# A hand-ordered setup of a fused attention and expert kernel: its steps and first loads in another order

## The reference

```python
mod = (silu(c) @ wmod).reshape(8, 6, 1, 256)       # six vectors a batch
sa, ca, ga, sb, cb, gb = (mod[:, i] for i in range(6))
ga = (2 * (ga >= 0) - 1) * maximum(abs(ga), 0.25)  # the gates, gb alike
h = layernorm(x) * (1 + ca) + sa
x = x + ga * attention(h, ...)   # q = (h w_dq^T) w_uq^T and a rotated part through w_qr,
                                 # k, v = (h w_dkv^T) through w_uk, w_uv, rotated k = h w_kr^T;
                                 # causal softmax over 512 keys, then w_out
h = layernorm(x) * (1 + cb) + sb
x = x + gb * ffn(h, ...)         # top 8 of 32 experts merged into 8 groups of width 96
```

## Time and profile before

| | us |
|---|---|
| median of 3 runs (lowest, highest) | 1097.45 (1093.78, 1107.73) |
| the profiled execution's own time | 1096.97 |
| its span in the trace | 1095.0 |
| PE busy | 1026.2 (94%) |
| DVE busy | 771.5 (70%) |
| ACT busy | 401.1 (37%) |
| POOL busy | 412.7 (38%) |

### The profile page before, as it was taken

One profiled execution on the slowest core, in us unless ns is written; L12 is line 12 of the kernel. 1 busy time (PEld: TensorE's weight loads), 2 busy tenths in 40 slices (PEclk: granted clock), 3 DMA queues, 4 the chain that ended last, 5 costly groups with the idle time before them and its releaser, 6 DMA issues.

```text
span 1095.0 us, 24777 instructions
## 1 busy us (share of the span) xinstructions
PE 1026.2 (94%) x9744; PEld 730.9 (67%) x9744; DVE 771.5 (70%) x1516; ACT 401.1 (37%) x723; POOL 412.7 (38%) x349
## 2 busy tenths in 40 slices
PE   6979989999999989999899999999999998999778
PEld 4646667766677667766677666776677666776456
DVE  5767687585957868677885859678686777857344
ACT  3334533254314443145332543144431453314310
POOL 1526442264505353154422644054441544226100
PEclk9989999999999999999999999999999999999979
DMA  6220000200002000200002000020002000010000
GB/s 191 58 88 2 2 1 1 68 2 2 1 4 67 2 1 1 69 2 2 1 1 69 2 2 1 2 69 2 1 1 69 2 2 1 1 49 2 1 1 20
DMA packets 22232, 23.59 MB, mean 22 GB/s; under 512 B 6314, under 2 KB 20138, under 8 KB 22130
## 3 DMA queue, kind: packets, MB, share of 16 engines
q1 hardware_dynamic: 22130, 22.02, 6.6%
HBM read 17.80 MB, written 4.21 MB: 20 GB/s over the span
## 4 chain that ended last, share of the span: by engine, by line
PE 82%; DVE 11%; issue 4%; ACT 2%; POOL 1%; DMA 1%; POOLq 0%; DVEq 0%; SPq 0%; ACTq 0%
PE ring L1131 17%; PE ring L981 12%; PE ring L982 10%; PE ring L983 10%; PE ring L1203 8%; PE av L1147 7%; PE ring L1107 6%; PE ring L1098 3%; DVE mcol L863 2%; DVE xr L902 1%; PE ring L1115 1%; PE ring L1192 1%; DVE prod L839 1%; PE av L1160 1%; PE ring L1042 1%
## 5 line engine op out<-in xcount | busy, mean ns | idle before, releaser
L672 ACT ACTIVATE pt<-ring 128x384 f32<-128x384 f32 (+1 forms) x384 | 170.9, 532 | 326.2 <-PE ring L1131 289.7
L562 POOL TENSOR_SCALAR_AFFINE_SELECT pt<-pt 128x512 f32<-128x512 f32 x128 | 79.4, 635 | 409.6 <-ACT pt L672 409.6
L863 DVE TENSOR_REDUCE mcol<-ring 128x1 f32<-128x128 f32 (+3 forms) x512 | 212.3, 483 | 19.3 <-PE ring L1107 18.1
L839 DVE TENSOR_TENSOR prod<-ring,table 128x1024 f32<-128x1024 f32 x128 | 155.4, 1219 | 93.1 <-PE ring L983 92.5
L1131 PE MATMUL ring<-rows 32*128 32x512 f32 (+3 forms) x3072 | 175.9, 330 | 9.4 <-ACT pt L672 4.9
L1131 PEld LDWEIGHTS ring<-rows 32*128 32x128 f32 x3072 | 130.4, 184 | 60.6 <-issue 35.0
L553 POOL TENSOR_TENSOR rows<-prod,rows 128x1024 fp32r<-128x1024 f32 x64 | 152.5, 2393 | 36.3 <-ACT rows L652 36.3
L546 POOL TENSOR_TENSOR prod<-prod 128x512 f32<-128x512 f32 x64 | 82.5, 1290 | 134.3 <-DVE prod L839 133.7
L652 ACT ACTIVATE rows<-prod 128x1024 fp32r<-128x1024 f32 x64 | 67.0, 1060 | 60.2 <-PE ring L1131 39.3
L1147 PE MATMUL av<-pt,vals 128*17 128x512 f32 (+3 forms) x1024 | 85.3, 439 | 3.2 <-POOL pt L562 3.2
L1131 PE MATMUL ring<-cont 32*128 32x512 f32 (+3 forms) x1024 | 85.6, 319 | 0.0
(11 more groups left out here) (162 smaller groups left out, 1624.4 us busy)
## 6 DMA issues: line engine op xcount, KB each, us to landing
xn<-x_dram SPq DMA_DIRECT2D x8, 512.0 KB, 4.1
...
dn<-wu_t_dram SPq DMA_DIRECT2D x1, 640.0 KB, 10.1
...
```

The source lines that it names most:

```text
L672: sc.activation(pt[:, PT_AT[n] + h * w:PT_AT[n] + (h + 1) * w], ps[:, 0:w], ACT.Exp, scale=SCALE).then_inc(exp_ready.sem, 1)
L839: ve.tensor_tensor(prod[:, s % PROD, :, :], ps[:, :].unsqueeze(1).broadcast_to([P, 2, S]), table[:, :, :], ALU.mult).then_inc(rotated.sem, 1)
L863: last = ve.reduce_max(mcol[:, q, h * HR + HD:h * HR + HD + 1], ps[:, at:at + (q + 1) * P], AX_X)
```

## The change

The setup list becomes one table, and three things move. `spread` goes to the front; the sixteen steps and the rest are in a new order, with `fuse.0` behind the first two `rope` steps, both `values` last, and `fuse.4`, `fuse.5` among the `maxima`. The gates' five DVE instructions become two steps, `gates_out` (the two that read PSUM) and `gates_end` (the other three), far apart. The loads of the query weights are divided in columns 0 to 511 and the rest, the rest behind the small loads with a semaphore of its own. The two tiny `groups` loads go to places two and three of SP's queue, ahead of `c_t` and `wmod`. SP waits for the PE part of `gates` where it waited for DVE's read of it. No arithmetic changes.

```diff
@@ the list (a line or two of it; the moves stand below) @@
-latent.0 latent_hi.0 latent_lo.0 fuse.1 rope.0000 rotate.0000 rope.0001 rotate.0001 combine.000 kcon.00 kcon_hi.00
...
+modulate1.01 low1.01 latent.0 latent_hi.0 latent_lo.0 rope.0000 rope.0001 rotate.0000 rotate.0001 combine.000
+gates_out. fuse.0 hi.000 fuse.1 rope.0010 rotate.0010 lo.000 rope.0011 rotate.0011 split_uv. combine.001 kcon.00
...
-def setup_steps():
-    out = [("silu",), ("stats1", 0), ("pow1", 0), ("norm1", 0), ("mod",), ("split_d",), ("split_k",), ("turn1", 0, 0), ("turn1", 0, 1),
-           ("gates",), ("modulate1", 0, 0), ("low1", 0, 0), ("modulate1", 0, 1), ("low1", 0, 1), ("fuse", 0), ("split_uv",)]
-    return out + steps_of(SETUP_ORDER)
...
             sp.dma_start(idx_sb[:, :], chosen).then_inc(ld_idx, 16)
+            for copy in range(2):
+                sp.dma_start(grp_i[copy * NX:(copy + 1) * NX, :], groups).then_inc(ld_idx, 16)
             sp.dma_start(ct[:, :, :], c_t.rearrange("(c p) b -> p c b", p=P)).then_inc(ld_mod, 16)
...
-            sp.dma_start(wu_main, wu_t[0:P, :]).then_inc(ld_q, 16)
-            sp.dma_start(wu_rest, wu_t[P:CQ, 0:NG * NROPE]).then_inc(ld_q, 16)
-            sp.dma_start(wu_rest_con, wu_t[P:CQ, NG * NROPE:NQ]).then_inc(ld_q, 16)
+            sp.dma_start(wu_main[:, 0:512], wu_t[0:P, 0:512]).then_inc(ld_q, 16)
+            sp.dma_start(wu_rest[:, 0:512], wu_t[P:CQ, 0:512]).then_inc(ld_q, 16)
...
-                sp.dma_start(grp_i[copy * NX:(copy + 1) * NX, :], groups).then_inc(ld_small, 16)
             sp.dma_start(gw_st, gw_t.rearrange("(c p) n -> p c n", p=P)).then_inc(ld_small, 16)
+            sp.dma_start(wu_main[:, 512:], wu_t[0:P, 512:NQ]).then_inc(ld_rest, 16)
+            sp.dma_start(wu_rest[:, 512:], wu_t[P:CQ, 512:NG * NROPE]).then_inc(ld_rest, 16)
+            sp.dma_start(wu_rest_con, wu_t[P:CQ, NG * NROPE:NQ]).then_inc(ld_rest, 16)
...
-            sp.wait_ge(gates_read, 1)
+            sp.wait_ge(full_sem, full_value(0, "setup", PLACES["setup"][0][("gates",)]))
...
-                    elif kind == "gates":
+                    elif kind == "gates_out":
...
                         ve.sem_inc(gates_read, 1)
+                    elif kind == "gates_end":
                         chain(ve.scalar_tensor_tensor(gates_abs, gates_abs, -1.0, gates_abs,
...
                         if step[1] == 0:
-                            pe.wait_ge(ld_q, 80)
+                            pe.wait_ge(ld_q, 64)
+                        if step[1] == EC:
+                            pe.wait_ge(ld_rest, 48)
...
+                        if isinstance(b, int) and b == 0 and g == 2 and t == 1:
+                            pe.wait_ge(fuse_read, len(FUSE))
...
                         if part == "setup":
-                            pe.wait_ge(fuse_read, len(FUSE) if g else 2 * EC)
+                            pe.wait_ge(fuse_read, 2 * EC)
```

More of the change, by code:

```diff
@@ L68, in steps_of @@
         kind, args = token.split(".")
-        out.append((kind, *map(int, args)))
+        out.append((kind, *(int(i) for i in args)))
     return out
 SETUP_ORDER = """
-latent.0 latent_hi.0 latent_lo.0 fuse.1 rope.0000 rotate.0000 rope.0001 rotate.0001 combine.000 kcon.00 kcon_hi.00
-kcon_lo.00 rope.0010 rotate.0010 rope.0011 rotate.0011 hi.000 lo.000 combine.001 fuse.2 fuse.3 hi.001 lo.001
-rope.0100 rotate.0100 qcon.00 qcon_hi.00 qcon_lo.00 rope.0101 rotate.0101 combine.010 values.00 values_out.00
-values.01 values_out.01 kcon.01 kcon_hi.01 kcon_lo.01 hi.010 maxima.000 reduce.000 lo.010 rope.0110 rotate.0110
-maxima.001 reduce.001 rope.0111 rotate.0111 combine.011 maxima.002 reduce.002 fuse.4 fuse.5 qcon.01 qcon_hi.01
-qcon_lo.01 shift.00 shifted.00 hi.011 lo.011 spread. split_ffn.0 split_ffn.1
+spread. silu. stats1.0 pow1.0 split_d. norm1.0 mod. split_k. turn1.00 turn1.01 gates. modulate1.00 low1.00
+modulate1.01 low1.01 latent.0 latent_hi.0 latent_lo.0 rope.0000 rope.0001 rotate.0000 rotate.0001 combine.000
+gates_out. fuse.0 hi.000 fuse.1 rope.0010 rotate.0010 lo.000 rope.0011 rotate.0011 split_uv. combine.001 kcon.00
+kcon_hi.00 kcon_lo.00 rope.0100 rope.0101 fuse.2 fuse.3 hi.001 lo.001 rotate.0100 rotate.0101 combine.010 qcon.00
+qcon_hi.00 qcon_lo.00 maxima.000 reduce.000 fuse.4 hi.010 rope.0110 rotate.0110 rope.0111 rotate.0111 combine.011
+lo.010 gates_end. maxima.001 reduce.001 fuse.5 split_ffn.0 kcon.01 kcon_hi.01 kcon_lo.01 qcon.01 qcon_hi.01
+qcon_lo.01 hi.011 lo.011 split_ffn.1 maxima.002 reduce.002 shift.00 shifted.00 values.00 values_out.00 values.01
+values_out.01
 """
@@ L144, in ring_places @@
     return place, n
-SETUP, FIRST, LAST = setup_steps(), steps_of(BODY_ORDER), steps_of(LAST_ORDER)
+SETUP, FIRST, LAST = steps_of(SETUP_ORDER), steps_of(BODY_ORDER), steps_of(LAST_ORDER)
 PLACES = {}
@@ L251, in block_program @@
         av = ctx.enter_context(nc.psum_tensor("av", [P, 512], F32))
-        ld_wo, ld_d, ld_mod, ld_q, ld_k, ld_tab, ld_small, ld_ffn, ld_down, ld_idx = (
-            sem(n) for n in ("ld_wo", "ld_d", "ld_mod", "ld_q", "ld_k", "ld_tab", "ld_small", "ld_ffn", "ld_down", "ld_idx"))
+        ld_wo, ld_d, ld_mod, ld_q, ld_rest, ld_k, ld_tab, ld_small, ld_ffn, ld_down, ld_idx = (
+            sem(n) for n in ("ld_wo", "ld_d", "ld_mod", "ld_q", "ld_rest", "ld_k", "ld_tab", "ld_small", "ld_ffn", "ld_down", "ld_idx"))
         x_loaded = Count(sem("x_loaded"), 1, 16)
@@ L325, in block_program @@
         cst_ready = sem("cst_ready")
-        N_SMALL = 7
+        N_SMALL = 5
         def full_value(b, part, place):
@@ L466, in _ @@
                       .then_inc(ld_tab, 16)
-            sp.wait_ge(ld_idx, 16)
+            sp.wait_ge(ld_idx, 48)
             sp.wait_ge(mod_read, 1)
-            sp.wait_ge(gates_read, 1)
+            sp.wait_ge(full_sem, full_value(0, "setup", PLACES["setup"][0][("gates",)]))
             chosen_at = [sp.value_load(idx_sb[0:1, g:g + 1], min_val=0, max_val=NX - 1) for g in range(G)]
@@ L757, in program @@
                         last.then_inc(mod_ready, 1)
-                    elif kind == "gates":
-                        ps = wait_full(ve, b, part, step)
+                    elif kind == "gates_out":
+                        ps = wait_full(ve, b, part, ("gates",))
                         ve.wait_ge(keys_split, 1 + EC)
@@ L770, in program @@
                     elif kind == "spread":
-                        ve.wait_ge(ld_small, 16 * N_SMALL)
+                        ve.wait_ge(ld_idx, 48)
                         ve.wait_ge(pool_setup, 4)
```

## The result

The change makes the kernel slower: **1112.08 us** median of 20 runs (1107.14 to 1113.85) against 1097.42 (1092.20 to 1107.92, 20 runs). The ratio is 1.0111, 95% interval 1.0086 to 1.0137: under 2%, but clear of no change. The profiled execution took 1113.46 us with a span of 1111.4, against 1096.97 and 1095.0: 16.4 us more of span.

What follows compares the result with a forecast made beforehand. PE was taken to bound the kernel, busy 1026 of 1095 us, so only setup waits and low clock could change. Setup balance +2.5 plus 0.5 for the clock, +3 us on 1096.97, gave 1100.0, range 1093 to 1106.

Steps and rivals of the forecast that it cites:

- DVE's queue: Setup, first maxima to shift: 17.1 us of DVE work plus 1.5 of waits ends at 68.1; PE stands still 7.5 us.
- the clock of the give-back: PE's lower clock behind the new pauses and at the front: 0.5 us taken for both, 0 to 2.6 kept.
- The loads: Kernel start: two `groups` issues ahead of `wmod` make PE begin at 10.1, +1.1 us.
- The front: Early setup: `latent` starts at 22.5, 2.8 us earlier, and `combine.000` at 28.0, 6.7 us earlier.
- The give-back: Setup up to `maxima.000`: PE pauses of 2.1, 2.9 and 1.6 us turn the 6.7 us lead into a 1.4 loss.
- takes some 1.6 (the pair shown 1.12 ...): `split_uv` on DVE ahead of `kcon.00`: pair 1.12 us plus two smaller operations estimated at 0.5, so PE waits 2.9.
- 67 to 70: Sign of a wrong forecast: DVE's last setup reduction, forecast to end at 68.1 us, ending outside this range.
- 2 us of waits: Sign of a wrong forecast: DVE's queue behind `maxima.000` having more waits than this; 1.5 us was forecast.
- The clock behind the shift: Behind PE's 7.5 us pause: a 1.2 GHz stretch as long as before's 6.8 us, losing 3.2, so no difference.
- If the body, not the setup, moved by more than 3 us: Sign of a wrong forecast: the unchanged work behind the setup was expected to keep its length.
- third rival: Loop: clock falls in all eight batches, not four, adding four 1.6 us stretches, +6.4; 1103 to 1108 us, chance 0.15.
- first two rivals: Clock does not fall or falls half as long, 1096 to 1098, chance 0.15; 6.7 us lead kept, 1085 to 1091, 0.1.

Runs made afterwards that it cites:

- o0: The changed code and loads with the setup list of the kernel before: 1099.52 us, ratio 1.0024 to the kernel before.
- a1: The changed kernel with only `split_uv` moved, to right behind `low1.01`: 1104.20 us, ratio 1.0044 to the kernel before.
- a3: The changed kernel with `split_uv` behind `low1.01`, and `gates_end` and both halves of `split_ffn` behind the values: 1096.97 us, ratio 1.0009 to before.
- a2: The changed kernel with `gates_end` and both halves of `split_ffn` moved behind the values: 1104.67 us, ratio 1.0050 to the kernel before.
- o2: The changed code and loads with the list of the kernel before, but `spread` first: 1104.23 us, ratio 1.0039 to before.
- p1: The changed code with the list of before, `spread` first, plus five extra POOL subtractions beside it on an unread tile: 1107.37 us, one run.
- best1: The changed code with the front of before, `spread` first, gates' chain divided, half of `split_ffn` early, `groups` loaded behind `xn`: 1102.71 us, ratio 0.9997 to before.
- u1: The changed kernel with `split_uv` one place earlier on DVE, ahead of the product of `rope.0011`: 1101.24 us, ratio 1.0030 to before.

## Why the prediction was wrong

The forecast was 1100.0, within 1093 to 1106; it is 1112. In the setup the mechanism stood: the order of the list wins in the front, gives it back at three places that were named, and DVE's queue then holds PE ahead of the shift. Three of its terms were too small: `split_uv`, the clock of the give-back, and DVE's queue. And nearly half of the loss is in the loop, for which the sum had nothing.

*The loads.* +1.1 forecast, 9.73 against 8.97 measured: +0.8. `mod` at 9.73 is just outside the mark that the prediction set itself, 10.1 within 0.3. o0, with the same loads, shows no loss further on.

*The front.* `latent` 21.96 (forecast 22.5), combine 27.73 (28.0). Right, though by the trace `latent` still waits 1.20 us for DVE: PE was quicker through `gates` (2.31 for 3.5) than priced.

*The give-back.* Forecast: pauses of 2.1, 2.9 and 1.6 us, `maxima.000` ready at 49.5. Measured: 2.23, 4.83 and 1.61, ready at 55.2, 5.7 us later. **The step that failed is "takes some 1.6 (the pair shown 1.12 ...)"**: the duration came from a row of before in which POOL was idle, while at the new place POOL runs the combine that DVE's product before it has just released. `split_uv` took 3.5 us there (38.50 to 42.02) and not 1.6, which makes 1.9 us. **The second step that failed is "I take 0.5 for both, and keep 0 to 2.6"**: the clock took 3.8. It is low for 3.4 us behind the first pause, 1.6 lost, and for 6.8 around the second, of which 4.7 with work on PE, 2.2 lost (by 0.23 / 0.43 of the earlier trace rows). 1.9 + 1.6 + 2.2 = 5.7. a1 removes both stretches with `split_uv`'s place alone, but it keeps the first pause, so that the pause brings the first stretch is not shown.

*DVE's queue.* Forecast 17.1 us of work and 1.5 of waits; measured 55.51 to 75.52, 20.0, nearly all work. The same fault: L767, L768 and the second half of `split_ffn` are each 1.0 us longer beside POOL, 2.9 in all, and the waits are 0.6 and not 1.5. The end is 7.4 us late: 6.0 from above and 1.4 here. So the last reduction ended at 75.52, outside the 67 to 70 that the prediction had named as its own sign of being wrong. The bound "2 us of waits" was no bound on what was wrong, since a stretched operation reads as work.

*The clock behind the shift.* The forecast took a low stretch as long as before's, 6.8 us with work in it, 3.2 lost, and so no difference. It is 10.2 us long, but 5.0 of them lie in the pause, where nothing is lost. Behind it PE works 5.1 us at 0.50 and loses 2.4: from the pause's end to the scores it took 6.5 us, forecast 4.1. So here after loses 0.8 us less than before does.

The setup's sum from these parts: 2.5 forecast without the clock, + 1.9 for `split_uv`, + 3.8 for the clock of the give-back, + 0.3 for the later start of DVE's queue, + 1.4 for the queue, - 0.8 = 9.1. The marker says 9.1.

*The loop.* "If the body, not the setup, moved by more than 3 us" was named as what would prove the forecast wrong, and it did: +7.3. That is the third rival's mechanism, but not as it was put. It counted 1.6 us for each of four more batches, 6.4; there are five stretches of 6.8 us for four of 3.4, 20.4 us more at 0.50, which by 0.23 / 0.43 can cost up to 9.5. Nor was it rare, as the chance of 0.15 has it: 14 of 20 runs of after have a mean clock of 0.968 or less, at 1111.4 us or more. That the body's length is the clock's the profiled executions of all the kernels show, as it goes with the us at 0.50 in the loop: 1009.3 to 1010.5 us at 6.8 and 10.2, 1011.2 at 13.7 (before, a3), 1018.5 and 1018.7 at 34.1 (after, a2), 1022.7 to 1022.9 at 47.8. The 16.4 us of the profiled execution are thus 9.1 + 7.3. Putting four of the moved steps elsewhere (a3) takes back both. That the order *causes* the bad loop was not shown: o2, p1 and best1, with short setups, had it too in the profiled execution, with 6.8 us in all seven batches (47.8 us), and u1, with the long setup, had not. What decides it stays open.

*The range* ended at 1106 because the clock of the give-back was bounded by one stretch of 3.4 us, no duration was let grow at its new place, and the loop was left to a rival. The first two rivals played no part.
